# Routing of a mixture-of-experts block: softmax and top experts per group in the mixer rounds, slot products in fp32r and in eight lots

## The reference

```
probs = softmax(x @ Wr)                       # 32 experts, per token
topw, topi = top_k(probs, 4); topw /= sum(topw)
shared = silu(x @ Wsg) * (x @ Wsu) @ Wsd * sigmoid(x @ Wse)       # 1408 wide
pos = place of the pair (token, expert) in its expert's queue
      # a running count over all pairs, in the order of the tokens
xe[expert, pos] = x[token]   if pos < 64
ye = (silu(xe @ Wg) * (xe @ Wu)) @ Wd         # per expert, 352 wide
out[token] = shared + sum over its 4 experts of topw * ye[expert, pos]
```

## Time and profile before

| | |
|---|---|
| median of 3 runs | 819.86 us (818.2 to 820.6) |
| profiled execution: its own time, its span | 820.32 us, 818.5 us |
| TensorE matmul, weight load | busy 725.8 us (89%), 508.7 us (62%) |
| VectorE, ScalarE, GpSimd | busy 418.1 us (51%), 244.0 us (30%), 208.9 us (26%) |
| mean granted clock of TensorE | 0.918 |
| mixer rounds | 0 to 269 us |
| units 3, 4, 5 | 269 to 297, to 339.5, to 388 us |
| units 6 to 11 with the pairs | 388 to 690 us |
| units 12 to 15 with the combination | 690 to 818.5 us |

### The profile page before, as it was taken

The page is one execution under the profiler, slowest core; times in us unless marked ns, Lnnn a source line. Parts: engine busy times, 40 slices in busy tenths (PEclk is TensorE's granted clock), DMA queues, the critical chain, the costliest instruction groups (busy, mean ns, idle before and its releaser), DMA issues.

```text
span 818.5 us, 9071 instructions
## 1 busy us (share of the span) xinstructions
PE 725.8 (89%) x3345; PEld 508.7 (62%) x3345; DVE 418.1 (51%) x747; ACT 244.0 (30%) x442; POOL 208.9 (26%) x200
## 2 busy tenths in 40 slices
PE   4878779979979886799999989999799999896995
PEld 3655557757737664689665656556366566784774
DVE  3767756627646584671332342322223325687777
ACT  2333554444342341120121422213113133422420
POOL 0252722523503102000100000000000002788881
PEclk9799868989969997986999999999999999998998
DMA  8640000000004003000778776777878872521111
GB/s 286 222 157 1 27 26 14 26 14 14 37 2 167 1 0 116 0 1 1 243 270 310 270 268 238 272 269 270 321 252 280 294 265 97 162 70 40 40 40 65
DMA packets 48152, 111.46 MB, mean 136 GB/s; under 512 B 9056, under 2 KB 13172, under 8 KB 48108
## 3 DMA queue, kind: packets, MB, share of 16 engines
q1 hardware_dynamic: 41708, 102.46, 35.0%
q0 software_dynamic: 6400, 8.42, 3.6%
HBM read 110.83 MB, written 12.58 MB: 151 GB/s over the span
## 4 chain that ended last, share of the span: by engine, by line
PE 54%; DVE 12%; issue 10%; DMA 9%; POOL 7%; ACT 5%; SPq 2%; POOLq 0%; DVEq 0%; ACTq 0%
PE bank L1549 18%; PE bank L1604 8%; PE bank L1561 7%; DMA egu<-in_L_ffn_Wu_dram 5%; PE bank L1621 4%; PE bank L1501 4%; DMA expert_rows<-ye 3%; PE bank L1512 3%; PE bank L1653 3%; POOL egu L642 2%; PE bank L1532 2%; PE bank L1521 1%; DMA xres<-in_L_attn_x_dram 1%; PE bank L1452 1%; DVE ytmp L1267 1%
## 5 line engine op out<-in xcount | busy, mean ns | idle before, releaser
L1549 PE MATMUL bank<-xsH,wguH 128*128 128x512 f32 x352 | 144.4, 410 | 8.6 <-DVE xsL L1129 5.0
L1549 PE MATMUL bank<-xsH,wguL 128*128 128x512 f32 x352 | 139.5, 396 | 0.0
L1549 PE MATMUL bank<-xsL,wguH 128*128 128x512 f32 x352 | 139.4, 396 | 0.0
L624 POOL DMA_INDIRECT xg<-h_rows,slot_tok x16 | 15.4, 963 | 325.2 <-PE bank L1592 250.0
L1561 PE MATMUL bank<-wdH,prodH 128*128 128x512 f32 x176 | 78.8, 448 | 20.5 <-DVE prodL L1139 9.5
L1549 PEld LDWEIGHTS bank<-xsH,wguH 128*128 128x128 f32 x352 | 67.5, 192 | 35.6 <-issue 14.7
L1604 PE MATMUL bank<-egu,xeT 128*64 128x352 f32 x512 | 80.8, 469 | 9.5 <-DMA egu<-in_L_ffn_Wu_dram 9.3
L1137 DVE TENSOR_TENSOR prod<-bank,silu 128x512 f32<-128x512 f32 x38 | 26.2, 690 | 101.3 <-PE bank L1549 92.8
L1549 PEld LDWEIGHTS bank<-xsL,wguH 128*128 128x128 f32 x352 | 67.4, 191 | 14.8
L1549 PEld LDWEIGHTS bank<-xsH,wguL 128*128 128x128 f32 x352 | 67.4, 191 | 13.4 <-issue 0.5
L1561 PE MATMUL bank<-wdL,prodH 128*128 128x512 f32 x176 | 73.6, 418 | 0.0
(11 more groups left out here) (227 smaller groups left out, 1121.2 us busy)
## 6 DMA issues: line engine op xcount, KB each, us to landing
egu<-in_L_ffn_Wg_dram SPq DMA_DIRECT2D x32, 704.0 KB, 6.6
egu<-in_L_ffn_Wu_dram SPq DMA_DIRECT2D x32, 704.0 KB, 7.6
ed<-in_L_ffn_Wd_dram SPq DMA_DIRECT2D x32, 512.0 KB, 5.5
h2T<-in_L_wmod_dram SPq DMA_DIRECT2D x6, 1024.0 KB, 8.6
ed<-in_L_ffn_Wd_dram SPq DMA_DIRECT2D x32, 192.0 KB, 6.5
xres<-in_L_attn_x_dram SPq DMA_DIRECT2D x4, 1024.0 KB, 10.5
h_rows<-ho SPq DMA_DIRECT2D x16, 256.0 KB, 2.0
expert_rows<-ye SPq DMA_DIRECT2D x16, 256.0 KB, 7.3
```

The costliest lines, as they stand in the source:

```text
L1549: ins = mm.matmul(bk[:, :], l[f][:, w, c, :], r[:, c, :], start=(k == 0), stop=(k == 3 * C - 1))
```

## The change

The shift by the maximum, Exp, the scaling and the search for the 8 largest and their indices are done group by group: for group g - 2 in round g of the mixer (rounds 2 to 4), on a quarter of the columns, and for group 3 at the end of the mixer rounds and in unit 3. The softmax stays in the tile `logits`. `top8`, `top_i` and `rmax` get tiles of their own. The one-hot rows move from unit 4 to unit 3, the scan to the start of unit 4, the count products one chunk forward, and VectorE's `positions` is cut into `counts_picked` and the sum. The comparison tiles `hot0` to `hot2` and the ids are fp32r, so the slot products are; the 64 products are issued in eight lots of eight: lots 0 and 1 around the last half of unit 5, lots 2 to 5 behind its down products, lots 6 and 7 in unit 6. `pair_ids`, the calls of `slots_of`, `slot_table` and `slot_weights` move later. The pair stages start three places later. `tri`, `ones` and the iotas lie in the tile `xeT`.

```diff
-        PAIRS_FROM = (6, 2)
+        PAIRS_FROM = (6, 5)
...
+                hot2 = sb("hot2", [P, GT * TOP_K, P], F32R, routing)
...
+                ids = sb("ids", [P, NT * TOP_K, NP], F32R, routing)
...
-        probs = scr[:, 0:NT * E].rearrange("p (i e) -> p i e", e=E)
+        probs = logits[:, :, 0:E]
...
+        at_slot = (hot0, hot1, hot2)
...
ScalarE:
+                def exps(g):
+                    act.wait_ge(shift_ok, g + 1)
+                    at = slice(g * GT, (g + 1) * GT)
+                    a.activation(probs[:, at, :], probs[:, at, :], ACT.Exp).then_inc(ex_ok, 1)
...
+                        if g >= 2 and i == 0:
+                            exps(g - 2)
...
                 split_group(0, EARLY)
-                act.wait_ge(shift_ok, 1)
-                a.activation(probs, probs, ACT.Exp).then_inc(ex_ok, 1)
+                exps(EARLY)
...
VectorE, mixer rounds:
                             lo_group(0, g - 2)
                             sigma_of(g - 2)
+                            shifted_logits(g - 2)
...
+                        if g >= 2 and i == 2:
+                            top_experts(g - 2)
                         if g < NG:
                             mix_front(t)
...
VectorE, units:
+                        if u == ROUTE and f == 0:
+                            pairs_before()
+                        if u == ROUTE + 2 and f == 1:
+                            slot_table()
                         gate_up(p, g, f)
                         if u == EARLY and f == 0:
-                            top_experts()
+                            top_experts(EARLY)
                         if u == EARLY and f == 1:
-                            experts_of()
+                            experts_ones()
...
-                        if u == ROUTE and f == 0:
-                            experts_ones()
                         if u == ROUTE and f == 1:
-                            pairs_before()
+                            counts_picked()
                         if u == ROUTE and f == 2:
                             positions()
                         if u == ROUTE + 1 and f == 0:
                             slots()
+                        if u == ROUTE + 1 and f == 1:
                             pair_ids()
-                        if u == ROUTE + 1 and f == 1:
                             slots_of(0)
+                        if u == ROUTE + 1 and f == 2:
                             slots_of(1)
-                        if u == ROUTE + 1 and f == 2:
                             slots_of(2)
+                        if u == ROUTE + 2 and f == 0:
                             slots_of(3)
+                        if u == ROUTE + 2 and f == 1:
+                            slot_weights()
...
TensorE:
+                def slot_tokens(s):
+
+                    q, k0 = s // 2, s % 2 * 8
                     pe.wait_ge(at_ok, q + 1)
...
+                    for k in range(k0, k0 + 8):
                         ins = mm.matmul(tokB, at_slot[q % 3][:, k, :], ids[:, q * n + k, :],
...
                         half(p, g, f, 0)
                         pair_stages(u, 2 * f)
-                        if u == ROUTE and f == 2:
+                        if u == ROUTE and f == 1:
                             positions()
+                        if u == ROUTE + 1 and f == 2:
+                            slot_tokens(0)
+                        if u == ROUTE + 2 and f == 1:
+                            slot_tokens(7)
                         half(p, g, f, 1)
                         pair_stages(u, 2 * f + 1)
-                    if u == ROUTE + 1:
-                        slot_tokens(0)
-                        slot_tokens(1)
+                        if u == ROUTE + 1 and f == 2:
+                            slot_tokens(1)
+                        if u == ROUTE + 2 and f == 0:
+                            slot_tokens(6)
                     for m in range(GT):
                         down(p, g, m)
-                        if u == ROUTE + 1 and m in (0, 1):
+                        if u == ROUTE + 1:
                             slot_tokens(m + 2)
```

More of the change, by code:

```diff
@@ L104, in build @@
         sigma = sb("sigma", [P, NT])
+        top8 = sb("top8", [P, NT, 8])
+        top_i = sb("top_i", [P, NT, 8], U32)
+        rmax = sb("rmax", [P, NT])
         NC0 = PARTS[0]
@@ L185, in build @@
             prodL += [sb("prodL2", [P, GW], F32R, pb)]
+            with ExitStack() as routing:
+                sb("pad0", [P, 512], F32, routing)
+                hot2 = sb("hot2", [P, GT * TOP_K, P], F32R, routing)
+                sb("pad1", [P, 672], F32, routing)
+                hot1 = sb("hot1", [P, GT * TOP_K, P], F32R, routing)
+                sb("pad2", [P, 352], F32, routing)
+                hot0 = sb("hot0", [P, GT * TOP_K, P], F32R, routing)
+                ids = sb("ids", [P, NT * TOP_K, NP], F32R, routing)
             egu = sb("egu", [P, 2, 2, C, F], F32, pb)
@@ L219, in build @@
         keep = scd[:, 0:NT * E].rearrange("p (e i) -> p e i", e=E)
[L222 to L227, removed]
+        at_slot = (hot0, hot1, hot2)
+        ids_i = ids[:, :, :].rearrange("p (i k) h -> p i (k h)", i=NT)
+        pair_hot = scd[:, 2048:3072].rearrange("p (n h) -> p n h", h=NP)
+        pair_hot_i = scd[:, 2048:3072].rearrange("p (i n) -> p i n", i=NT)
+        tri, ones, iota_r, iota_w = (xeT[:, c, :] for c in range(C))
+        iota_w = iota_w.bitcast(U32)
         id_f = scr[:, 5536:5536 + NT]
@@ L1169, in over_e, with shifted_logits, top_experts @@
                 def over_e(ap):
[L1170 to L1178, removed]
-                    link(v.tensor_reduce(rmax[:, :], probs, AX.X, ALU.add))
-                    link(v.reciprocal(rmax[:, :], rmax[:, :]))
-                    link(v.tensor_tensor(probs, probs, over_e(rmax[:, :]), ALU.mult))
-                    for i in range(NT):
+                    return ap.rearrange("p (i a) -> p i a", a=1).to_broadcast([P, GT, E])
+                def shifted_logits(g):
+                    at = slice(g * GT, (g + 1) * GT)
+                    product_taken(dve, ("router", g))
+                    link(v.tensor_reduce(rmax[:, at], probs[:, at, :], AX.X, ALU.max))
+                    v.tensor_tensor(probs[:, at, :], probs[:, at, :], over_e(rmax[:, at]), ALU.subtract).then_inc(shift_ok, 1)
+                def top_experts(g):
+                    at, tiles = slice(g * GT, (g + 1) * GT), range(g * GT, (g + 1) * GT)
+                    dve.wait_ge(ex_ok, g + 1)
+                    link(v.tensor_reduce(rmax[:, at], probs[:, at, :], AX.X, ALU.add))
+                    link(v.reciprocal(rmax[:, at], rmax[:, at]))
+                    link(v.tensor_tensor(probs[:, at, :], probs[:, at, :], over_e(rmax[:, at]), ALU.mult))
+                    for i in tiles:
                         v.max(top8[:, i, :], probs[:, i, :]).then_inc(dve_self, 1)
@@ L1185, in top_experts @@
                     dve.wait_ge(dve_self, own.last())
-                def experts_of():
-                    for i in range(NT):
+                    for i in tiles:
                         v.max_index(top_i[:, i, :], top8[:, i, :], probs[:, i, :]).then_inc(dve_self, 1)
@@ L1206, in pairs_before, with counts_picked @@
                     v.tensor_tensor_scan(flat_ei(upto), flat_ei(keep), flat_ei(mask), 0.0, ALU.mult, ALU.add).then_inc(scan_ok, 1)
-                def positions():
+                def counts_picked():
                     dve.wait_ge(pos_full, 1)
@@ L1323, in _ @@
                         sigma_of(EARLY)
+                        shifted_logits(EARLY)
                         for m in range(2, GT):
```

25 lines of the change are left out of this document (8 added, 17 removed).

## The result

The changed kernel takes 833.0 us (median of four runs, 830.9 to 835.1) against 820.2 us for the kernel before: a ratio of 1.0158, 95% interval 1.0124 to 1.0193. The prediction was 815.2 us and its range ended at 822; it was wrong in sign. The profiled execution took 830.91 us for a span of 829.1 us, 10.6 us more than before in both; it is the fastest of the four.

A forecast was written before the change was run, and what follows sets the result against it. It took units 3 to 5 as the reserve, held by GpSimd's additions, the scan, slot products and the first pair's weights. First load -3.3 and pair units -1.4 give -4.7 us: 819.86 to 815.2 us, range 807 to 822.

The forecast's parts named there:

- Drops 1.9: Unit 5: slow products behind the new waits cost 1.9 us, one term of the 38.0 us expected for the unit.
- signs of being wrong: Mixer rounds over 10 us later at 269 us; low clock through units 5 and 6; egu waits staying near 9 us.
- waits of 2.4 us or more: TensorE: each such wait is followed by slow products worth 1.2 to 2 us; waits under 1 us are not.
- the count products then run at full clock (3.8 to 1.7 us): Unit 4: with the 6.7 us wait gone, these products take 1.7 us instead of 3.8, within a gain of 12.8 us.
- TensorE's 2.9 us wait for ytmp stays: Unit 3: one-hot comparisons (2.5 us) replace index searches (2.6 us), so this wait keeps its length; unit total -5.5 us.
- under unit 3's down products: Units 3 and 4: GpSimd's additions run beside unit 3's down products, removing unit 4's 6.7 us wait.
- Mixer rounds, +7.5: Rounds 2, 3 and last: VectorE steps, table change and clock drops cost 7.5 us in all, bounds 4.5 and 10.
- +22.1: Unit 6: slot weights ready 22.1 us into the unit, so pair weights may start at 388.8 us instead of 392.1.
- -1.4: Pair units: 9.0 us of shared products done ahead, less 7.6 us more waiting for weights; bounds -9.0 and +3.
- rival 1: Pair units: the transfers' round trip doesn't bind and the 9.0 us come through; 807.6 us, chance 0.17.
- Rival 3: Mixer rounds eat the gain: six table changes of 1.28 us all on the chain; 821.6 us, chance 0.20.
- Rival 2: Units 5 and 6: the lots hold the clock down, 84 products 0.2 us slower each; 829 us, chance 0.11.

The follow-up runs named there:

- run 3: Changed kernel with pair ids, masks, slot table and slot weights back in their old places in unit 5, pair units from place (6, 2): 803.9 us, ratio 0.976.
- run 9: Changed kernel with 16 extra products, result unused, on TensorE ahead of lot 0 and again ahead of lot 6: 822.5 us, ratio 1.002.
- run 4: Changed kernel with, in the mixer rounds, Exp ahead of the gate chunk on ScalarE and the top experts at the end of step 0 on VectorE: 822.0 us.
- run 5: Changed kernel with only VectorE's slot steps moved one chunk sooner, lots and everything behind them left in place: 809.8 us, ratio 0.985.
- run 1: Kernel before with only the softmax and top experts per group in the mixer rounds; slot products fp32, in lots of 16: 822.6 us, ratio 1.002.
- run 8: Changed kernel with only ScalarE's Exp moved ahead of the gate chunk in the mixer rounds: 831.1 us, ratio 1.012.
- run 11: The kernel of run 10 with the top experts of all four groups moved to unit 3: 800.2 us, ratio 0.975 to the kernel before.
- run 7: Changed kernel with the moves of run 3 and run 4 together: 801.9 us, ratio 0.975.
- run 6: The kernel of run 5 with lots 2 to 7, slot weights and slot table also early in unit 5, pair units from place (6, 2): 802.9 us.
- run 12: The kernel of run 6 with the four slot tiles in fp32 instead of fp32r: 816.3 us, ratio 0.996 to the kernel before.
- run 2: Kernel before with only the three masks and the ids in fp32r tiles: 808.7 us, ratio 0.983.
- run 10: Changed kernel with the moves of run 6 and run 4 together: 794.8 us, ratio 0.967.

## Why the prediction was wrong

By the prediction's own steps, in the profiled spans, with a last line for all that lies behind the start of unit 6. The prediction has unit 5 end at 388.1 us before, 1.9 us too early. It forecast the unit's new length and the time of the first load from products and waits, so its sum doesn't change. But against the real edge its -10.6 reads -12.6, and its 16.7 behind it (21.4 - 3.3 - 1.4) reads 18.7:

| step | predicted | measured |
|---|---|---|
| ahead of the first router product | 0 | +2.9 |
| mixer rounds | +7.5 | +10.3 |
| unit 3 | -5.5 | -4.3 |
| unit 4 | -12.8 | -9.6 |
| unit 5 | -12.6 | -7.9 |
| start of unit 6 to the end | +18.7 | +19.2 |
| sum | -4.7 | +10.6 |

The step that failed is the price of the low clock behind the new waits, "Drops 1.9" in unit 5, where 6.7 us were measured. The waits and most other mechanisms were right. The first line is chance; four sizes were off, all to the same side, and unit 5 is the largest miss. Part of the miss is chance too: 2.9 us of start-up, the 2.6 us at the end of the rounds that runs 3 and 9 don't have, and the 3.2 us of unit 5 that run 4 doesn't have. Taken off the profiled span, these 8.7 us would leave it 1.9 us above before, by this estimate, still not 4.7 below. Two of the prediction's signs of being wrong came: unit 3 starts 13.2 us later, and the clock is 0.84 and 0.88 in units 5 and 6.

**Unit 5, "Drops 1.9".** The waits were foreseen: 4.15 us at lot 0 (4.22), 4.4 at lot 6 (4.43), 1.8 for ytmp (1.42). What they drag behind them was not. Run 5 shows 6.7 us of slow products in this unit alone and 4.0 in unit 6; run 9 takes part of it back by mere filling. The rule "waits of 2.4 us or more" was read off a stretch with few waits: here a wait of 1.42 us, 15.5 us after another, is followed by a lot of 1.71 us and nine products in 3.98, though in run 4 the same wait is not. The sum put 38.0 us; it was 42.7.

**Unit 4, "the count products then run at full clock (3.8 to 1.7 us)".** They don't get faster. This is the first pair of records after:

```profile
314.44 1.88 PE L1663 MATMUL bank<-ed,xeT 128*128 128x512 f32 x2
```

The window from 314 to 318 us has the granted clock at 1.00 and 4.00 us busy. I had halved a number that wasn't clock: the fp32 product of 512 columns is two records of 0.85 us from start to start at full clock. The two products took 3.75 us before and take 3.44 now, where the sum had 1.7: 1.7 of the 3.2 us missed. Another 0.6 is the clock drop credited behind the ytmp wait. The wait fell from 4.84 to 2.53 us as foreseen, but the products behind it are as slow as before, some 1.5 us in all:

```profile
333.10 0.80 PE L1581 MATMUL bank<-wdH,prodH 128*128 128x512 f32 x1 [2.53 <-DVE ytmp L1171]
333.69 0.63 PE L1581 MATMUL bank<-wdL,prodH 128*128 128x512 f32 x1
```

A short wait for xsL at 307.5 us and the slower products around it give 0.5 more.

**Unit 3, "TensorE's 2.9 us wait for ytmp stays".** It grew to 3.91 us, because VectorE's split now takes 2.35 us where it took 1.29, and GpSimd's additions now run beside it. In run 1, where they don't, the same split takes 1.29 us. VectorE's timeline and GpSimd's:

```profile
298.08 2.35 DVE L1142 TENSOR_TENSOR xsL<-h2T,xsH 128x512 fp32r<-128x512 f32 x2
...
301.13 1.25 DVE L1174 TENSOR_TENSOR xres<-xres,ytmp 128x512 f32<-128x512 f32 x1
```

```profile
298.25 1.64 POOL L624 TENSOR_TENSOR ed<-egu 128x512 f32<-128x512 f32 x1 [16.72 <-DVE egu L1210]
```

I had moved the additions "under unit 3's down products" at no price; the xres addition takes 0.69 us elsewhere.

**Mixer rounds, +7.5.** The durations on VectorE were right, against the earlier trace rows:

```profile
L1202 DVE FIND_INDEX8 top_i<-top,logits 128x8 uint32<-128x32 f32 x16 | 2.7, 185 | 0.0
...
L1196 DVE TENSOR_TENSOR logits<-logits,rmax 128x128 f32<-128x128 f32 x4 | 1.2, 293 | 0.1
L1188 DVE TENSOR_REDUCE rmax<-logits 128x4 f32<-128x128 f32 x4 | 1.1, 286 | 0.1
L1194 DVE TENSOR_REDUCE rmax<-logits 128x4 f32<-128x128 f32 x4 | 1.1, 276 | 0.0
```

From the router column on, the key/value products of round 2 start 2.6 us later and those of round 3 3.6 (2.0 and 2.9 foreseen, without the drops). The last round has 6.7 more, not 3.0. Of the 10.3 in all, 1.4 are the table loads (run 8; 1.6 foreseen) and 8.9 the top experts (runs 8 and 11), of which the sum had 5.9 with all its clock drops. The last round contains the 12 us at a clock of 0.58 shown under run 7. Where that clock was full, in runs 3 and 9, the rounds are 7.6 to 7.7 us longer than before: the predicted 7.5. So here the sum was right for one of two outcomes of the same instructions.

**Unit 6, "+22.1".** The slot weights came 23.9 us into the unit, and the first load 13.2 us later than before instead of 3.3 sooner. That 18.1 us of TensorE's gain (20.0 by the real edge of unit 6) would go into work ahead of the first load was the prediction's own sentence. It isn't what makes the change a loss: run 5 leaves that order and comes to 809.8 us, and undoing it in run 6 gives 6.9 us more.

**Pair units, "-1.4".** From the issue of the first load to the end it is 423.8 us, before 426.4: -2.6. TensorE waits 16.1 us for pair weights, foreseen 19.3; rival 1 (7.6 us more won) did not come. So all of the miss lies ahead of the first load.

**The rivals.** Rival 3 gave 821.6 us by six table changes on the chain. The profile has the six more loads:

```profile
L798 ACT ACT_TABLE_LOAD x7 | 9.0, 1283 | 3.0 <-DVE prodL L1152 2.0 <-issue 1.0
L759 ACT ACT_TABLE_LOAD x3 | 3.8, 1283 | 0.1
```

Run 8 takes all six away and wins 1.4 us. So the rounds do eat some of the gain, but not by the tables. The rule of the Trainium skill ("ScalarE: Activation LUTs", Rules for kernel authors), to finish one set before a switch, holds in sign and is small here. Its budget of about 2.7 us a switch is more than the trace shows: a load takes 1.283 us, and in the kernel after it is 1.32 us from the end of a silu (196.05 us) to the start of the Exp behind the load (197.37 us). Rival 2 had nearly the right number (829 us) and half the mechanism: a low clock through units 5 and 6, but set off by the waits, not by the lots. With fp32 lots it comes closer: in run 12, in another order of the steps, the lots do bring the clock down, from 366 us to the end of unit 5. The chance of 0.11 was too low, since rival 2 asked for 84 slow products in one stretch, and I did not count the same loss in pieces.

Left open: 2.2 us more between the medians (12.8) than between the profiled executions; where the start-up's 2.9 us come from; and why the clock at the end of the last round, and behind the second wait of unit 5, is sometimes full with the same instructions.

## What to carry to other kernels

Put a product behind the last step that feeds it on the other engine's list, with a margin of one chunk: two waits of 4 us, with the low clock and the later first load behind them, cost 23 us here: without them nearly the same order of work takes 809.8 us instead of 833.0. When a wait is priced, price the products behind it at the lower clock as well, and allow for short waits too. Take more than one profile before you give a few us a cause: three stretches differed by about 3 us each with the same instructions. Before halving a duration for the clock, look at a window's granted clock and at the records of one product, and split a change into its parts: the types of the slot tiles were worth 11.8 us, while the rest of the change spent more than that.

## What the runs showed that I had not expected

- fp32 slot products lower TensorE's clock though it never idles: from 1.00 to 0.50 between 362 and 370 us in run 12, with 4.00 of 4.00 us busy. The same lots in fp32r leave it at 1.00 (run 6). So fp32r saves 16 to 18 us in unit 5 of the profiles (runs 2 and 12) for 64 products, of which about 7, an estimate, follow from one record instead of two (0.9 a lot).
- Behind the same wait of 1.42 us in unit 5 there is a stretch of low clock in the kernel after and in runs 8 and 9, and none in run 4. The waits of 0.99 us in runs 5, 6 and 10 have none behind them.
- Work that nobody needs can shorten a kernel: with 32 unused products (7.6 us of TensorE) units 5 and 6 together are 5.5 us shorter.
- VectorE's subtraction and addition of two tensors of 512 columns take 1.07 to 1.25 us beside a GpSimd addition, 0.69 alone. The ytmp step between them, which reads one operand from a PSUM bank, stays at 0.74 us.
